# The first outer tap of a convolution: from VectorE to ScalarE and Pool

## The reference

```python
def bit_linear(x, w):            # x quantised per token, w to -1, 0, 1
    return jnp.einsum('bsd,hd->bsh', act_quant(x), weight_quant(w))
h = bit_linear(x, w1)                                    # 256 -> 1024
h = depthwise_conv1d(h.transpose(0, 2, 1), conv_w, conv_b)   # 3 taps along the tokens, padding 1
h = jax.nn.silu(h.transpose(0, 2, 1))
return bit_linear(h, w2)                                 # 1024 -> 256
```

## Time and profile before

| | |
|---|---|
| median of 3 runs | 2816.32 us (2815.0 to 2820.91) |
| profiled execution, its own time | 2818.34 us |
| its span, first to last instruction | 2816.6 us |
| TensorE busy | 2333.1 us (83%) |
| VectorE busy | 1941.5 us (69%) |
| ScalarE busy | 1471.4 us (52%) |
| Pool busy | 1035.7 us (37%) |
| mean granted clock of TensorE | 0.903 |

### The profile page before, as it was taken

How to read it: one execution, slowest core, us unless ns; L and a number is a source line. 1 busy time by engine, 2 the same in 40 slices (tenths; PEclk the granted TensorE clock), 3 DMA queues, 4 the chain that set the end, 5 groups by cost and what they waited for, 6 DMA issues and landing times. The chain is left out here.

```text
span 2816.6 us, 43303 instructions
## 1 busy us (share of the span) xinstructions
PE 2333.1 (83%) x16184; PEld 1911.5 (68%) x16184; DVE 1941.5 (69%) x4456; ACT 1471.4 (52%) x2446; POOL 1035.7 (37%) x1011
## 2 busy tenths in 40 slices
PE   4778888877589999999975999999999956767575
PEld 2445455554377888888865999999999935445444
DVE  4698888895355666666654666676666647978877
ACT  2457777664355565565452544444455435454543
POOL 3243444432132344443453444454444432213030
PEclk9789988886789999999987999999999978888887
DMA  8600000000100001100014555555555320001000
GB/s 266 229 1 17 4 14 16 8 9 8 33 16 1 26 28 44 48 31 21 17 50 142 112 126 141 137 116 134 141 133 130 65 52 11 31 11 31 0 16 15
DMA packets 144472, 171.03 MB, mean 61 GB/s; under 512 B 16920, under 2 KB 114053, under 8 KB 144264
## 3 DMA queue, kind: packets, MB, share of 16 engines
q1 hardware_dynamic: 114360, 136.15, 14.7%
q0 software_dynamic: 29184, 31.99, 7.8%
q10 hardware_dynamic: 720, 0.12, 0.0%
HBM read 100.73 MB, written 74.32 MB: 62 GB/s over the span
## 5 line engine op out<-in xcount | busy, mean ns | idle before, releaser
L2191 POOL DMA_INDIRECT x_after_l<-rowsout,target x160 | 266.6, 1666 | 319.6 <-DVE rowsout L2317 261.5
L162 PE MATMUL SC<-Xhi,Whi 128*128 128x320 f32 x1024 | 321.7, 314 | 6.6 <-DVE HF L2359 3.6
L162 PE MATMUL SC<-Xhi,Wlo 128*128 128x320 f32 x1024 | 317.5, 310 | 0.0
L162 PE MATMUL SC<-Xlo,Whi 128*128 128x320 f32 x1024 | 317.3, 310 | 0.0
L645 POOL TENSOR_TENSOR PR<-PR,rs 128x616 f32<-128x616 f32 x128 | 163.2, 1275 | 390.4 <-DVE rs L1039 390.4
L1406 POOL TENSOR_TENSOR ff_Hlo<-ff_HF,ff_Hhi 128x512 fp32r<-128x512 f32 x108 | 143.2, 1326 | 387.8 <-ACT ff_Hhi L1539 387.8
L2288 ACT ACTIVATE SG<-SC 128x320 f32<-128x320 f32 x256 | 111.9, 437 | 237.3 <-PE SC L162 235.9
L2324 DVE TENSOR_TENSOR Hlo<-HF,Hhi 128x320 fp32r<-128x320 f32 x256 | 129.7, 507 | 104.3 <-ACT Hhi L2276 104.3
L162 PEld LDWEIGHTS SC<-Xhi,Whi 128*128 128x128 f32 x1024 | 193.4, 189 | 10.1 <-DVE HF L2359 7.2
L1808 DVE TENSOR_TENSOR ff_HF<-ff_HG,SC 128x512 f32<-128x512 f32 x112 | 76.7, 685 | 172.6 <-ACT ff_HG L1533 112.9
L162 PEld LDWEIGHTS SC<-Xlo,Whi 128*128 128x128 f32 x1024 | 193.5, 189 | 0.0
(11 more groups left out here) (498 smaller groups left out, 6874.4 us busy)
## 6 DMA issues: line engine op xcount, KB each, us to landing
expert_in<-zeros SPq DMA_DIRECT2D x4, 5440.0 KB, 35.7
rowsin<-expert_in SPq DMA_DIRECT2D x32, 680.0 KB, 4.5
first_expert<-L_wg SPq DMA_DIRECT2D x16, 512.0 KB, 5.4
first_expert<-L_wu SPq DMA_DIRECT2D x16, 512.0 KB, 6.4
first_expert<-L_wd SPq DMA_DIRECT2D x16, 512.0 KB, 7.4
Wraw<-L_wg SPq DMA_DIRECT2D x16, 512.0 KB, 5.5
Wraw<-L_wu SPq DMA_DIRECT2D x16, 512.0 KB, 6.4
Wraw<-L_wd SPq DMA_DIRECT2D x16, 512.0 KB, 7.3
```

Of the source, the lines that this page charges most:

```text
L162: last = nc.tensor.matmul(out, lhs[l], rhs[r], start=start and n == 0, stop=stop and n == 2)
L2191: nc.gpsimd.indirect_dma_start(x1rows[:, :], bass.IndirectOffsetOnAxis(ap=target[j % 2][:, t:t + 1], axis=0), rowsout[j % 2][:, t, :], Non ...
```

## The change

The operation on line 2742 (first outer tap, on VectorE, out of PSUM) is taken out, together with the wait behind it. In its place ScalarE multiplies the first tap: right behind Z of block h it writes first tap x `SC[h % 2]` into a tile in SBUF, `tap[h % 2]`. Pool adds this tile, shifted by one token, to the block's `Z`, after VectorE has added the other outer tap. A new semaphore, `tap_added`, counts Pool's additions; Silu waits for it instead of for `z_ready`, and so does the tap of block h for the addition of block h-2, whose tile it takes over. `Z` has three tiles instead of two. The new tiles lie in `OT` and `PT`. ScalarE's list now has, for block h: Z of block h, tap of block h, Silu of block h-2; the last two Silus follow behind the loop. The lists of TensorE and SyncE are not changed.

```diff
--- before.py
+++ after.py
@@ -2398,7 +2398,8 @@
 
         XQ = [[sb(f"XQ{part}_{g}", [P, KC, TOK], f32r) for part in ("hi", "lo")] for g in range(G)]
         X = [two(f"X3{i}", [P, TT, D]) for i in range(2)]
-        Z = two("Z", [P, S])
+        Z = two("Z", [P, S]) + [T["OT"][0][:, :, :].rearrange("p k n -> p (k n)")]
+        tap = [T["OT"][1][:, :, :].rearrange("p k n -> p (k n)"), T["PT"][0][:, :, :, :].rearrange("p a b c -> p (a b c)")[:, 0:S]]
         SL = sb("SL", [P, NHC, S])
         SQ = sb("SQ", [P, NHC, S], bf16)
 
@@ -2419,7 +2420,7 @@
                 "y_psum", "y_taken", "xqt_psum", "sx_ready", "xr_ready", "xq_ready", "xq_high", "xq_low", "h_psum", "z0_ready", "z_ready", "s_ready",
                 "am_ready", "tile_psum", "tile_taken", "s2_psum", "s2_ready", "q_ready", "o_psum", "o_ready",
                 "x_bias")}
-            vchain, ctx_in, kv_ready = (sa.one("l3_" + n) for n in ("vchain", "ctx_in", "kv_ready"))
+            vchain, ctx_in, kv_ready, tap_added = (sa.one("l3_" + n) for n in ("vchain", "ctx_in", "kv_ready", "tap_added"))
 
             with nc.Block() as block:
                 @block.sync
@@ -2471,6 +2472,10 @@
                                 pool.wait_ge(sm["ot_psum"][g], UNITS * (b + 1))
                             pool.wait_ge(ctx_in, CTX_IN * (b + 1))
                             last_layer_context(nc.gpsimd, L, headof, blockhead).then_inc(kv_ready, 1)
+                        for h in range(NHC):
+                            z = Z[h % 3]
+                            pool.wait_ge(sm["z_ready"][h % 2], b * HALF + h // 2 + 1)
+                            nc.gpsimd.tensor_tensor(z[:, 1:S], z[:, 1:S], tap[h % 2][:, 0:S - 1], ALU.add).then_inc(tap_added, 1)
 
                 @block.scalar
                 def _(act):
@@ -2502,8 +2507,8 @@
                         last.then_inc(sm["xr_ready"][g], 1)
 
                     def silu(b, p):
-                        act.wait_ge(sm["z_ready"][p % 2], b * HALF + p // 2 + 1)
-                        nc.scalar.activation(SL[:, p, :], Z[p % 2][:, :], ACT.Silu).then_inc(sm["s_ready"][p % 2], 1)
+                        act.wait_ge(tap_added, b * NHC + p + 1)
+                        nc.scalar.activation(SL[:, p, :], Z[p % 3][:, :], ACT.Silu).then_inc(sm["s_ready"][p % 2], 1)
                     for g in range(G):
                         root(g, 0, 1)
                     for g in range(G):
@@ -2527,12 +2532,16 @@
                             nc.scalar.activation(XQ[g][0][:, :, :].rearrange("p k n -> p (k n)"), GP[g][:, :], ACT.Copy).then_inc(sm["xq_high"][g], 1)
                         for h in range(NHC):
                             act.wait_ge(sm["h_psum"][h % 2], b * HALF + h // 2 + 1)
-                            if b or h >= 2:
-                                act.wait_ge(sm["s_ready"][h % 2], b * HALF + h // 2)
-                            nc.scalar.activation(Z[h % 2][:, :], SC[h % 2][:, :], ACT.Identity, bias=cbc[:, h:h + 1], scale=cwc[:, h, 1:2])\
+                            if h >= 3:
+                                act.wait_ge(sm["s_ready"][(h - 3) % 2], b * HALF + (h - 3) // 2 + 1)
+                            nc.scalar.activation(Z[h % 3][:, :], SC[h % 2][:, :], ACT.Identity, bias=cbc[:, h:h + 1], scale=cwc[:, h, 1:2])
+                            if h >= 2:
+                                act.wait_ge(tap_added, b * NHC + h - 1)
+                            nc.scalar.activation(tap[h % 2][:, 0:S - 1], SC[h % 2][:, 0:S - 1], ACT.Identity, scale=cwc[:, h, 0:1])\
                                 .then_inc(sm["z0_ready"][h % 2], 1)
-                            if h:
-                                silu(b, h - 1)
+                            if h >= 2:
+                                silu(b, h - 2)
+                        silu(b, NHC - 2)
                         silu(b, NHC - 1)
                         if b + 1 < B:
                             for g in range(G):
@@ -2737,9 +2746,8 @@
 
                         for h in range(NHC + 2):
                             if h < NHC:
-                                z, y = Z[h % 2], SC[h % 2]
+                                z, y = Z[h % 3], SC[h % 2]
                                 dve.wait_ge(sm["z0_ready"][h % 2], b * HALF + h // 2 + 1)
-                                link(stt(z[:, 1:S], y[:, 0:S - 1], cwc[:, h, 0:1], z[:, 1:S], ALU.mult, ALU.add))
                                 stt(z[:, 0:S - 1], y[:, 1:S], cwc[:, h, 2:3], z[:, 0:S - 1], ALU.mult, ALU.add).then_inc(sm["z_ready"][h % 2], 1)
                             if h >= 2:
                                 i = h - 2
```

## The result

The changed kernel takes 2920.69 us in the median of 4 runs (2918.82 to 2924.78), the kernel before 2816.68 us in the runs beside it: a ratio of 1.0371, with a 95% interval of 1.0357 to 1.0386. The forecast was 2921 us. The span of the profiled execution grew from 2816.6 to 2919.4 us.

A forecast was written before the change was run, and what follows sets the result against it. VectorE was taken to bound the kernel, at 32.59 us a batch. With TensorE and ScalarE taking turns, a batch sums to 58.7 us, 104 us more in four: 2921 us, range 2877 to 2937.

The forecast's parts named there:

- The mechanism: Convolution: transposes(h-2), ahead of product(h+1), wait for a Silu behind Z(h), so TensorE and ScalarE take turns; 104 us more.
- The round: One hidden block between Z(3) and Z(7): ScalarE's and TensorE's parts add to 8.08 us, where it was 3.64.
- ScalarE's part: In each round, Z, tap, Silu and a hand-over take 3.30 us, in which TensorE idles.
- the lower end: A round with TensorE at the full clock: 6.34 us.
- the first rival: TensorE's full clock holds in the rounds: 2881 us in all, 64 more; chance 0.14.
- the second rival: Every round comes cold, TensorE at half clock: 2930 us in all, 114 more; chance 0.19.
- Mostly cold: The forecast's own case: TensorE's work comes mostly at half clock after its pause, a round of 8.08 us; chance 0.60.
- the three quarters between the two prices: TensorE's part of a round: three quarters of the way from 3.04 (full clock) to 5.36 (half clock), 4.78 us.
- Z(3): Start of block 3's Z, counted from Z(0): 15.94 us, with TensorE at half clock after idling almost 5 us.
- the end: From Z(7) to the end of a batch's last maximum, with Pool once on the path: 10.43 us.
- The hidden work: ScalarE's normalisations for the next batch stay covered, by at least 0.6 us, before the copy of the scales.
- The third rival: Waiting transposes don't hold the product back; ScalarE runs without pause, rounds of 3.25 us: 2819 us, no change; chance 0.05.

The follow-up runs named there:

- either list's reordering: Changed kernel with TensorE's transposes and VectorE's maximum one block later: 2818.37 us; or with ScalarE's Silu(h-2) ahead of Z(h) instead of behind the tap: 2820.8 us.
- two pooled blocks: Changed kernel with only blocks 3 and 6 tapped through ScalarE and Pool, and Silu(h-1) behind the tap: 2808.22 us, 0.9972 of the kernel before.
- The filled pause: Changed kernel with 24 needless TensorE transposes ahead of each wait for Silu: 2897.66 us.
- the kernel with the longer lag: Changed kernel with TensorE transposing block h-3, not h-2, behind product(h), VectorE's maximum following: 2818.37 us, 1.0001 of the kernel before.

## Why the prediction was right

**The mechanism** was named before any run, and the runs bear it out from three sides: the order without the operations costs 62 us, the operations with the distance kept cost nothing that the runs can tell (ratio 1.0001), and either list's reordering takes the loss back. That VectorE was the bound fits the kernel with two pooled blocks, where two operations of 1.28 us less made a batch 2.0 us shorter; in the changed kernel VectorE's 41 us are spared, and ahead of its tap it idles 3.4 to 4.4 us in each round.

**The round** was put at 8.08 us, between 6.34 and 8.66; it was 8.16 in the mean (7.53 to 8.63). ScalarE's part, put at 3.30 us, took 3.21 (2705.74 to 2708.95 in the first view). The granted clock of 0.69 is also that of the earlier layer's stretch; TensorE was busy 0.60 of the time here and 0.53 there. The filled pause shows the lower end to be true: 6.21 us. No round had the full clock throughout, which excludes the first rival. The second, the half clock in every round, came true for two rounds of four in each batch: 8.62 to 8.63 us, with the transposes and the product at the half clock from end to end, as in the view from 2700.32 to 2705.74. In the other two, 7.53 to 7.80 us, the clock changed inside TensorE's part: the transposes at 2708.95 began at the full clock (1.54 us for the eight instead of 1.97) and the product behind them ran at the half clock nearly to its end; a round later the transposes were cold and the clock rose within the product. So three bursts of four began cold, as the second rival has it for every one. "Mostly cold" was right, but the three quarters between the two prices were chosen and not derived, and that the mean came to 0.78 of the way is luck within those bounds.

**Two terms of the sum were too long.** Z(3) was put at 15.94 us and came at 14.84. The transposes did start cold after 4.67 us of idling, as was said, but the product behind them came to the full clock halfway:

```profile
2692.65 1.97 PE L2595 MATMUL GP<-ident,SL 128*128 128x128 f32 x8 [4.67 <-ACT SL L2511]
2694.28 0.78 PE L2585 MATMUL SC<-XQhi,w1q 128*128 128x512 f32 x1
...
2695.98 0.39 PE L2585 MATMUL SC<-XQhi,w1q 128*128 128x512 f32 x1
...
2697.11 1.21 ACT L2537 ACTIVATE Z<-SC,cbc,cwc 128x1024 f32<-128x1024 f32 x1 [4.51 <-PE SC L2585]
```

From the product's start to its Z it is 2.83 us, not 3.79. And the end was put at 10.43 us and took 9.51: the last transposes came at 1.07 us and not at the cold price of 1.94. Ahead of them stood the transposes of blocks 5 and 6, 3.33 us of work, and a pause of 0.64 us (the first of the two views of the ends above); the prediction had them behind a longer pause, as in the kernel before, where they waited 2.58 us for VectorE.

**One term was missing.** By these errors four batches cost 97.4 us and not 104.4. That the median is met to 1 us is luck: it is owed to the 5.4 us outside the convolution, which the prediction left out. In the chain of work that ended last, followed back from the last instruction (start, length, what), the second product (1024 -> 256) ahead of the third batch shows half of one of these steps: the same 32 matmuls for either half of the tokens, the first of them at a granted clock of 0.81 over its 8 us.

```profile
2604.39 4.92 PE GP L2575 x32
...
2611.39 3.60 PE GP L2575 x32
...
2617.55 2.37 PE GP L220 x10
```

Before the change both took 3.60 us in that batch, and the ten transposes of line 220, in the attention, 1.28 us; these make up another 1.09 us. So this is the clock again, at a place that the edit doesn't touch, and the same two lines are slow by as much ahead of the fourth batch. What brings it about stays open. The longer convolution alone doesn't: with Pool's addition made short a batch takes 56.6 us, and yet 96.9 and 93.8 us lie ahead of the third and the fourth, as in the kernel before (97.2 and 94.0); with two pooled blocks a batch takes 30.6 us, and 99.5 us lie ahead of the third.

**The hidden work stayed hidden.** In the three batches that are followed by another, ScalarE still waits 0.62 us for the first of the two spread scales (1.6 us before), and 4.6 us in the last, which has no normalisation ahead of it. So the normalisation is done in time, with just the 0.6 us to spare that the prediction gave as the least.

**The third rival's price**, 2819 us with both engines in step, was met by the kernel with the longer lag, 2818. There it was reached by reordering, and with batches of 32.9 to 35.3 us where the rival had 33.3; that TensorE would pass by waiting transposes, no run shows, and in the changed kernel it didn't: the product at 2710.14 in the first view, free from 2700.64, stood behind its transposes.

## What to carry to other kernels

When a step moves in one engine's list, write down for each other engine what now stands between its wait and the next thing that it gives back. Where two in-order lists each hold the other's input behind their own wait, the engines take turns, and no share of busy time foretells it. A step that adds latency between two engines needs the same added distance in the consumer's list. And what an operation spared on the bound is worth ends at the next bound: here four blocks of eight gave no more than two.

## What the runs showed of the hardware

Needless work made the changed kernel faster: 24 needless transposes in each pause raised the granted clock from 0.69 to 1.00 and cut a round from 8.16 to 6.21 us, 23 us in all, at 3 us lost at each batch's end. In the kernel with the order alone, with pauses of 2.24 us between bursts of some 4.5, the mean granted clock was 0.75. Transposes alone ran at the full clock too: those of the last block in a batch of the changed kernel took 1.07 us, 0.64 us behind 3.33 us of other transposes and with no product between, where eight took 1.97 after a pause of 3.25. Pool's addition of 128x1023 took 2.34 to 2.41 us in the changed kernel, whether or not one of VectorE's multiply-adds out of PSUM ran at the same time (it did in 8 of 32 blocks); the multiply-adds kept their 1.28 us. Neither slowed the other.
